# DVE levels in two halves with the first one compared on DVE, G rows issued singly, and POOL's seven levels compared and scaled on POOL

## The chip, the core and the metric

The kernel runs on one core of a Trainium2 chip. Its engines are TensorE (PE, matmul), VectorE (DVE), ScalarE (ACT), GpSimd (POOL) and SyncE (SP), which here issues all the DMAs. Each engine works through its own instruction list in order and waits on semaphores for the others. The metric is the device time of one execution in microseconds; lower is better.

## What is computed

Two linear layers in a row and a residual. The first layer's weights are quantised to a codebook of 32 values, after a LoRA product has been added. Cut to what matters:

```
cb = codebook / max(|codebook|);  scale = exp(scale_log)
lora_delta = lora_B @ lora_A * 0.5                       # 2048 x 2048, rank 64
normalized = (weight + lora_delta).reshape(O, I/128, 128) / scale
idx = searchsorted((cb[:-1] + cb[1:]) / 2, normalized)   # 31 thresholds
w_eff = (cb[idx] * scale).reshape(O, I) + lora_delta
h = x @ w_eff.T                                          # x: 4096 rows of 2048
out = x + h @ W_base.T + b_base + experts(h)             # rank-16 expert part
```

All data are float32. The LoRA rank dimension and the expert part are small against the two large products.

## The kernel before

**Tiling.** The kernel does not compute h. It forms G = w_eff.T times the base weights (with 24 more columns for the experts, 2072 in all) and multiplies x by G. G has 16 blocks of 128 rows, done in four groups of four. For group 0, the start-up loop of `startup()` converts eight halves of weights (q = 0 to 7, each 128 x 1024, two to a block) and multiplies each by eight rows of 128 x 2072 base weights (`rows`, five matmuls of a row into five PSUM banks, in float32). Behind it TensorE multiplies x by the four finished blocks, and the conversion of the other 24 halves runs in the background, paced by `Background`.

**One half of weights.** POOL adds the LoRA delta and multiplies by the reciprocal scale (`normalise`, lines 1288 and 1291). The quantisation is a sum over 31 thresholds of a step times (weight > threshold). ACT makes one-byte masks of 0 or 255 by a saturating activation (`unit`, line 918: `mk`, five buffers). DVE takes 24 of the thresholds, one instruction of 1024 columns each: mask times step plus the running sum `acc`, in PSUM (line 1115; the first one, line 1111, subtracts the weight from the mask's product). Seven thresholds are POOL's: ACT writes a mask of its own for them (`mp`, line 924), POOL scales it (line 1302, `tm`) and adds it to its partial sum `pp` (line 1315). The last DVE instruction of a half adds both sums and the lowest code (line 1122, semaphore `cl`). POOL then multiplies by the scale and adds the delta (`effective`, lines 1323 and 1325, semaphore `we`), behind DVE's first level of the next half. The last half of the loop is finished by DVE itself (`final_weights`).

**LoRA products.** 64 `wide` products of two matmuls (lines 682 and 683) go through one PSUM bank `pd`; each waits until the one before was copied out (semaphore `dl`), by DVE for the first four (line 1099), by ACT for the rest (line 906). SP writes each pair to DRAM and reads the deltas back (lines 496, 505). `delta_places()` says after which (q, j) each one stands.

**Order.** All engines go through one list of events, `walk()`: for each half the levels j = 0 to 23, with the rows of the half before at j = 7 and, at j = 3 of every second half from q = 3, `rows_out`: ACT copies the finished block of G (line 957) and DVE takes its low part (line 1149), which the next block's rows wait for. SP's loads of base weights have a ring of three buffers; a load waits for the row three places earlier. DVE waits for masks in pairs, so its level 3 waits for ACT's mask 4, which ACT writes behind its copies of `rows_out`.

## Time and profile before

| | |
|---|---|
| median of 3 runs | 2389.73 us (2389.25 to 2390.38) |
| profiled execution: span | 2389.1 us |
| busy: PE, DVE, ACT, POOL | 97%, 71%, 60%, 53% |
| base-weight rows of group 0 on PE (line 703) | 560 records, 207.6 us busy |
| idle of POOL before line 1323, for DVE | 173.6 us over the whole run |
| DMA | 442.58 MB, 185 GB/s on average |

The times outside the profile (runs) and its span differ by 0.6 us. Busy shares are means over stages with different limits: in the first 320 us the halves are converted while TensorE has gaps; from there on it is full up to the last stores. A float32 matmul has two records in the trace.

### The profile page before, as it was taken

The numbers are of one execution on the slowest core, as the hardware profiler recorded it, in microseconds if no ns is written. First come the engines' busy times: TensorE is split into PE (matmuls) and PEld (weight loads), VectorE is DVE, ScalarE is ACT, GpSimd is POOL, SyncE is SP. The second block draws the span as 40 slices with busy tenths as digits, with TensorE's granted clock in tenths as the row PEclk, the third lists the DMA queues.
The fourth block names the chain that finished last, engine by engine and source line by source line (L and its number), as shares of the span: only waits on it lengthen the run. The fifth ranks groups of instructions, "written<-read, shape, count | busy, mean of one in ns | idle before, by whom it ended". The sixth has DMA issues, their size and how long they took to land.

```text
span 2389.1 us, 30759 instructions
## 1 busy us (share of the span) xinstructions
PE 2318.9 (97%) x11678; PEld 2102.9 (88%) x11678; DVE 1708.0 (71%) x2021; ACT 1427.1 (60%) x1799; POOL 1270.6 (53%) x704
## 2 busy tenths in 40 slices
PE   3989899999999999999999999999999999999999
PEld 2445479999999999999999999999999989999998
DVE  8899998999978868777868967878873333333333
ACT  7999978989977656665646657566643321111111
POOL 6989847779874437777764436777760000111010
PEclk9989999999999999999999999999999999999999
DMA  5788854443343435766764436667664334545554
GB/s 198 272 274 277 309 208 162 162 166 141 138 149 114 118 116 197 238 230 225 234 219 123 119 105 200 222 232 238 221 208 128 102 96 161 197 180 198 185 195 152
DMA packets 121561, 442.58 MB, mean 185 GB/s; under 512 B 12818, under 2 KB 53330, under 8 KB 84562
## 3 DMA queue, kind: packets, MB, share of 16 engines
q1 hardware_dynamic: 121412, 440.61, 54.4%
q8 instruction: 92, 1.51, 0.3%
q14 instruction: 57, 0.47, 0.1%
HBM read 289.43 MB, written 151.13 MB: 184 GB/s over the span
## 4 chain that ended last, share of the span: by engine, by line
PE 91%; DVE 4%; ACT 3%; POOL 1%; issue 0%; DMA 0%; SPq 0%; DVEq 0%; POOLq 0%; ACTq 0%
PE m L777 20%; PE m L776 20%; PE m L778 20%; PE m L761 8%; PE m L762 8%; PE m L760 8%; PE m L703 4%; DVE acc L1115 3%; ACT mk L918 2%; PE m L806 1%; ACT mp L924 1%; PE pd L682 0%; DMA lb<-in_lb 0%; PE pd L683 0%; ACT ds L906 0%
## 5 line engine op out<-in xcount | busy, mean ns | idle before, releaser
L1115 DVE SCALAR_TENSOR_TENSOR acc<-mk,dj,acc 128x1024 f32<-128x1024 uint8 x736 | 944.9, 1284 | 91.6 <-ACT mk L918 72.1
L776 PE MATMUL m<-gh,xh 128*128 128x384 f32 (+2 forms) x2560 | 903.2, 353 | 0.0
L777 PE MATMUL m<-gl,xh 128*128 128x384 f32 (+2 forms) x2560 | 898.7, 351 | 0.0
L778 PE MATMUL m<-gh,xl 128*128 128x384 f32 (+2 forms) x2560 | 896.0, 350 | 0.0
L918 ACT ACTIVATE mk<-wr,bj 128x1024 uint8<-128x1024 f32 x768 | 843.8, 1139 | 0.7 <-DVE acc L1115 0.7
L776 PEld LDWEIGHTS m<-gh,xh 128*128 128x128 f32 x2560 | 481.6, 188 | 23.5
L778 PEld LDWEIGHTS m<-gh,xl 128*128 128x128 f32 x2560 | 480.9, 188 | 23.6
L777 PEld LDWEIGHTS m<-gl,xh 128*128 128x128 f32 x2560 | 481.4, 188 | 21.2
L1315 POOL TENSOR_TENSOR pp<-pp,tm 128x1024 f32<-128x1024 f32 x192 | 466.4, 2429 | 22.0
L1335 POOL TENSOR_TENSOR xl<-xw,xh 128x512 fp32r<-128x512 f32 x96 | 124.1, 1294 | 564.7 <-ACT xh L972 564.4
L1302 POOL TENSOR_SCALAR tm<-mp,dj 128x1024 f32<-128x1024 uint8 x224 | 258.1, 1152 | 246.5 <-ACT mp L924 235.6
L760 PE MATMUL m<-kh,wh 128*128 128x384 f32 (+2 forms) x936 | 328.8, 351 | 0.0
L762 PE MATMUL m<-kh,wl 128*128 128x384 f32 (+2 forms) x936 | 328.2, 351 | 0.0
L761 PE MATMUL m<-kl,wh 128*128 128x384 f32 (+2 forms) x936 | 328.0, 350 | 0.0
L1169 DVE TENSOR_TENSOR kl<-kw,kh 128x384 fp32r<-128x384 f32 (+2 forms) x234 | 189.1, 822 | 141.2 <-ACT kh L952 140.7
L1163 DVE TENSOR_TENSOR part<-m,part 128x384 f32<-128x384 f32 (+2 forms) x320 | 187.9, 587 | 131.5 <-PE m L778 130.4
L952 ACT ACTIVATE kh<-kw 128x384 fp32r<-128x384 f32 (+2 forms) x234 | 126.8, 548 | 251.8 <-DMA kw<-in_wb 251.2
L924 ACT ACTIVATE mp<-wr,bj 128x1024 uint8<-128x1024 f32 x224 | 255.1, 1139 | 0.1
L972 ACT ACTIVATE xh<-xw 128x512 fp32r<-128x512 f32 x128 | 80.1, 628 | 240.2 <-DMA xw<-in_x 240.2
L703 PE MATMUL m<-rows,wr 128*128 128x384 f32 (+2 forms) x560 | 207.6, 534 | 2.3 <-POOL wr L1325 1.5
L703 PEld LDWEIGHTS m<-rows,wr 128*128 128x128 f32 x560 | 112.2, 201 | 96.3 <-issue 50.6
L760 PEld LDWEIGHTS m<-kh,wh 128*128 128x128 f32 x936 | 175.8, 188 | 8.4 <-POOL wl L1329 0.2
(131 smaller groups left out, 1781.3 us busy)
## 6 DMA issues: line engine op xcount, KB each, us to landing
part<-part SPq DMA_DIRECT2D x192, 1036.0 KB, 6.7
rows<-in_wb SPq DMA_DIRECT2D x61, 1036.0 KB, 4.8
xw<-in_x SPq DMA_DIRECT2D x128, 256.0 KB, 3.2
out<-part SPq DMA_DIRECT2D x31, 1024.0 KB, 4.2
kw<-in_wb SPq DMA_DIRECT2D x138, 192.0 KB, 2.4
wr<-in_w SPq DMA_DIRECT2D x32, 512.0 KB, 8.8
dl<-delta SPq DMA_DIRECT2D x30, 512.0 KB, 5.9
delta<-ds SPq DMA_DIRECT2D x24, 512.0 KB, 3.2
```

The source lines that it names most:

```text
L703: done = e.matmul(R.m[c][:, 0:width(c)], R.wr[raw_of(q)][:, (t % 8) * 128:(t % 8 + 1) * 128], R.rows[r % 3][:, cols(c)], start=t == 0, sto ...
L760: e.matmul(bank[:, 0:w], high, kh, start=t == 0, stop=False)
L761: e.matmul(bank[:, 0:w], high, kl, start=False, stop=False)
L762: done = e.matmul(bank[:, 0:w], low, kh, start=False, stop=t == NB - 1 and not own(b, c))
L776: e.matmul(R.m[c][:, 0:w], xh, gh, start=k == 0, stop=False)
L777: e.matmul(R.m[c][:, 0:w], xh, gl, start=False, stop=False)
L778: done = e.matmul(R.m[c][:, 0:w], xl, gh, start=False, stop=stop and k == n - 1)
L918: e.activation(R.mk[k % NM], w, ACT.Identity, bias=R.bj[:, j:j + 1], scale=GROW).then_inc(S["mk"], 1)
L924: e.activation(R.mp[k % 2], w, ACT.Identity, bias=R.bj[:, NV + i:NV + i + 1], scale=GROW).then_inc(S["mp"], 1)
L1115: e.scalar_tensor_tensor(R.acc, R.mk[k % NM], R.dj[:, j:j + 1], R.acc, ALU.mult, ALU.add).then_inc(S["ac"], 1)
L1302: e.tensor_scalar(R.tm[scaled_level(q, i)], R.mp[k % 2], R.dj[:, NV + i:NV + i + 1], 0.0, ALU.mult, ALU.add).then_inc(S["tm"], 1)
L1315: e.tensor_tensor(R.pp, R.pp if i else R.wr[raw_of(q)], R.tm[scaled_level(q, i)], ALU.add).then_inc(S["pp"], 1)
```

## The change

1. A DVE level becomes two instructions of 512 columns (`HALVES`). Each waits for its own half of the level before, so for the instruction before the last one. The closing instruction is halved too, and `cl` counts two per half of weights.
2. The first level needs no mask: DVE compares the weights with the threshold and multiplies by the step (`tensor_scalar`, `is_gt`, `mult`), from SBUF into PSUM. ACT writes 23 masks per half for DVE.
3. POOL's seven levels need no mask either: POOL compares the float32 weights and multiplies by the step (`spare`). The sum starts with the first two scaled levels, so there are six adds instead of seven; the weight itself is no longer in either sum. ACT writes no `mp`. For the later halves (q from 8) the first of the seven goes into `pp` directly (`spare_base`).
4. `effective` waits for the closing halves themselves.
5. The eight rows of a half are events of their own, at j = 7, 10, 15, 17, 20, 23, 23, 23 (`ROW_AT`), on PE and on SP. For q = 3 to 7 the four LoRA products stand at j = 9, 14, 19, 23 instead of 3 to 6; two of half 2 move to half 1. The second and fourth of each of these halves are copied by DVE (`on_vector`).

```diff
@@ -25,9 +25,11 @@
 NJ = NC - 1
 NP = 7
 NV = NJ - NP
+NA, MK = NP - 1, NV - 1
+HALVES = (slice(0, H // 2), slice(H // 2, H))
 SPARE_AT = (0, 3, 6, 10, 13, 16, 19)
-FIRST_AT, EARLY_AT = (1, 3, 5, 8, 11, 14, 17), (0, 1, 3, 6, 10, 13, 16)
 NORM_AT, SPLIT_EVERY = 8, 6
+ROW_AT, LATE_UNITS = (7, 10, 15, 17, 20, 23, 23, 23), (9, 14, 19, 23)
...
@@ -82,8 +84,9 @@
     for q in range(2 * N0):
         for j in range(NV):
             yield ("unit", q, j)
-            if j == 7 and q:
-                yield ("rows", q - 1)
+            for k in range(8):
+                if ROW_AT[k] == j and q:
+                    yield ("row", q - 1, k)
             if j == 3 and q >= 3 and q % 2:
                 yield ("rows_out", (q - 3) // 2)
         yield ("effect", q)
...
 
-    late = [(0, j) for j in range(6, 22, 2)] + [(1, j) for j in range(1, 7)] + [(2, 3), (2, 4)]
-    late += [(q, j) for q in range(3, 2 * N0) for j in range(3, 7)]
+    late = [(0, j) for j in range(6, 22, 2)] + [(1, j) for j in (1, 2, 3, 4, 5, 6, 9, 14)]
+    late += [(q, j) for q in range(3, 2 * N0) for j in LATE_UNITS]
     late += [(q, j) for q in range(2 * N0, NQ) for j in range(5, NV, 3)]
     return dict(zip(late, range(NDELTA)))
 
@@ -363,7 +366,7 @@
 
 def on_vector(n):
 
-    return n < 4
+    return n < 4 or 16 <= n < 16 + 4 * (2 * N0 - 3) and n % 2 == 1
 
 
...
-        elif what == "rows":
-            for r in range(8 * at[0] + 3, 8 * at[0] + 11):
-                row(r)
-            if at[0] == 2 * N0 - 3:
+        elif what == "row":
+            row(8 * at[0] + 3 + at[1])
+            if at == (2 * N0 - 3, 7):
...
-    def rows(q):
-        b, h = q // 2, q % 2
...
+    def row(q, k):
+        b, t = q // 2, 8 * (q % 2) + k
+        r = NB * b + t
+        if k == 0:
+            e.wait_ge(S["we"], q + 1)
+        if q == 0 and k == 0:
             e.wait_ge(S["dl"], NARROW)
-        for t in range(8 * h, 8 * h + 8):
-            r = NB * b + t
-            e.wait_ge(S[f"r{r % 3}"], 16 * (r // 3 + 1))
-            for c in range(NCH):
...
     def unit(q, j):
-        k, w = NV * q + j, R.wr[raw_of(q)]
+        m, w = MK * q + j - 1, R.wr[raw_of(q)]
         if j == 0:
             e.wait_ge(S["n"], q + 1)
             if q == 0:
                 e.wait_ge(S["bk"], BOOK_READY)
-        if k >= NM:
-            e.wait_ge(S["ac"], k - NM + 1)
-        e.activation(R.mk[k % NM], w, ACT.Identity, bias=R.bj[:, j:j + 1], scale=GROW).then_inc(S["mk"], 1)
-        if j in mask_places(q):
-            i = mask_places(q).index(j)
-            k = NP * q + i
-            if k >= 2:
-                e.wait_ge(S["tm"], k - 1)
-            e.activation(R.mp[k % 2], w, ACT.Identity, bias=R.bj[:, NV + i:NV + i + 1], scale=GROW).then_inc(S["mp"], 1)
+        else:
+            if m >= NM:
+                e.wait_ge(S["ac"], summed((m - NM) // MK, (m - NM) % MK + 1))
+            e.activation(R.mk[m % NM], w, ACT.Identity, bias=R.bj[:, j:j + 1], scale=GROW).then_inc(S["mk"], 1)
...
     def unit(q, j):
-        k = NV * q + j
-        if q >= 2 * N0 or k == 0:
-            e.wait_ge(S["mk"], k + 1)
-        elif j % 2:
-            e.wait_ge(S["mk"], k + 1 + (j < NV - 1))
-        if j == 0:
-            if q:
-                e.wait_ge(S["cl"], q)
-            e.scalar_tensor_tensor(R.acc, R.mk[k % NM], R.dj[:, j:j + 1], R.wr[raw_of(q)], ALU.mult,
-                                   ALU.subtract).then_inc(S["ac"], 1)
-        else:
-            e.wait_ge(S["ac"], k)
-            e.scalar_tensor_tensor(R.acc, R.mk[k % NM], R.dj[:, j:j + 1], R.acc, ALU.mult,
+        w, m = R.wr[raw_of(q)], MK * q + j - 1
+        for h, at in enumerate(HALVES):
+            if j == 0:
+                if h == 0:
+                    e.wait_ge(S["n"], q + 1)
+                    if q == 0:
+                        e.wait_ge(S["bk"], BOOK_READY)
+                if q:
+                    e.wait_ge(S["cl"], 2 * q - 1 + h)
+                e.tensor_scalar(R.acc[:, at], w[:, at], R.u[:, 1:2], R.dr[:, 0:1], ALU.is_gt, ALU.mult).then_inc(S["ac"], 1)
+                continue
+            if h == 0 and q >= 2 * N0:
+                e.wait_ge(S["mk"], MK * q + j)
+            elif h == 0 and j % 2:
+                e.wait_ge(S["mk"], MK * q + min(j + 1, MK))
+            e.wait_ge(S["ac"], summed(q, j - 1) - 1 + h)
+            e.scalar_tensor_tensor(R.acc[:, at], R.mk[m % NM][:, at], R.dj[:, j:j + 1], R.acc[:, at], ALU.mult,
                                    ALU.add).then_inc(S["ac"], 1)
         if j == NV - 1:
-            e.wait_ge(S["ac"], k + 1)
-            if q < 2 * N0 - 1:
-                e.wait_ge(S["mk"], k + 2)
-            e.wait_ge(S["pp"], NP * (q + 1))
-            e.scalar_tensor_tensor(R.wr[raw_of(q)], R.acc, R.cn[:, 0:1], R.pp, ALU.add, ALU.add).then_inc(S["cl"], 1)
+            for h, at in enumerate(HALVES):
+                if h == 0:
+                    e.wait_ge(S["pp"], NA * (q + 1))
+                e.wait_ge(S["ac"], summed(q, j) - 1 + h)
+                e.scalar_tensor_tensor(w[:, at], R.acc[:, at], R.cn[:, 0:1], R.pp[:, at], ALU.add,
+                                       ALU.add).then_inc(S["cl"], 1)
 
     def final_weights():
...
 
+    def spare(q, i, to):
+        n = NV + i
+        e.tensor_scalar(to, R.wr[raw_of(q)], R.u[:, n + 1:n + 2], R.dr[:, n:n + 1], ALU.is_gt,
+                        ALU.mult).then_inc(S["tm"], 1)
+
+    def spare_base(q):
+        e.wait_ge(S["n"], q + 1)
+        e.wait_ge(S["cl"], 2 * q)
+        spare(q, 0, R.pp)
+
...
+
     def spare_scaled(q, i):
-        k = NP * q + i
-        e.wait_ge(S["mp"], k + 1)
-        if k == 0:
-            e.wait_ge(S["bk"], BOOK_READY)
+        if i == 0:
+            e.wait_ge(S["n"], q + 1)
+            if q == 0:
+                e.wait_ge(S["bk"], BOOK_READY)
         if q >= 2 * N0:
-            e.wait_ge(S["pp"], k)
-        elif k >= 2:
-            e.wait_ge(S["pp"], k - 1)
-        e.tensor_scalar(R.tm[scaled_level(q, i)], R.mp[k % 2], R.dj[:, NV + i:NV + i + 1], 0.0, ALU.mult, ALU.add).then_inc(S["tm"], 1)
+            e.wait_ge(S["pp"], NA * q + i - 1)
+        elif i in (2, 3):
+            e.wait_ge(S["pp"], NA * q + 1)
+        elif i > 3:
+            e.wait_ge(S["pp"], NA * q + i - 2)
+        elif q:
+            e.wait_ge(S["pp"], NA * q + i - 1)
+        spare(q, i, R.tm[scaled_level(q, i)])
 
     def spare_added(q, i):
         k = NP * q + i
-        if i == 0:
-            e.wait_ge(S["n"], q + 1)
+        if i == 1:
             if q:
-                e.wait_ge(S["cl"], q)
+                e.wait_ge(S["cl"], 2 * q)
             if q == 2 * N0:
                 e.wait_ge(S["rl"], NB // 2 - FINAL_WHOLE)
-        if i:
-            e.wait_ge(S["pp"], k)
+        else:
+            e.wait_ge(S["pp"], NA * q + i - 1)
         e.wait_ge(S["tm"], k + 1)
-        e.tensor_tensor(R.pp, R.pp if i else R.wr[raw_of(q)], R.tm[scaled_level(q, i)], ALU.add).then_inc(S["pp"], 1)
+        first = R.tm[scaled_level(q, 0)] if i == 1 and q < 2 * N0 else R.pp
+        e.tensor_tensor(R.pp, first, R.tm[scaled_level(q, i)], ALU.add).then_inc(S["pp"], 1)
 
     def effective(q):
         w = R.wr[raw_of(q)]
-        if q < 2 * N0:
-            e.wait_ge(S["ac"], NV * (q + 1) + 1)
-        else:
-            e.wait_ge(S["cl"], q + 1)
+        e.wait_ge(S["cl"], 2 * q + 2)
         e.tensor_tensor(grouped(w, 8), grouped(w, 8), per_group(R.sc, 8 * q, 8), ALU.mult).then_inc(S["ws"], 1)
         e.wait_ge(S["ws"], q + 1)
         e.tensor_tensor(w, w, R.dl[q % 2], ALU.add).then_inc(S["we"], 1)
...
                         spare_scaled(q, i)
-                else:
-                    if (q, i) == (0, 0):
+                        spare_added(q, i)
+                    elif q > 2 * N0:
+                        spare_base(q)
+                elif i == 0:
+                    if q == 0:
                         spare_scaled(0, 0)
                         spare_scaled(0, 1)
-                    if 1 < i + 1 < NP:
+                elif i == 1:
+                    spare_added(q, 1)
+                    spare_scaled(q, 2)
+                else:
+                    if i + 1 < NP:
                         spare_scaled(q, i + 1)
-                spare_added(q, i)
+                    spare_added(q, i)
             if j == NORM_AT and q + 1 < NQ:
                 normalise(q + 1)
             if at == (0, 11):
                 lora_b(1)
         elif what == "effect":
-            if at[0] < 2 * N0:
+            if at[0] < 2 * N0 - 1:
                 spare_scaled(at[0] + 1, 0)
-            if at[0] < 2 * N0 - 1:
                 spare_scaled(at[0] + 1, 1)
-            if at[0] != 2 * N0 - 1:
+            if at[0] == 2 * N0 - 1:
+                spare_base(2 * N0)
+            else:
                 effective(*at)
         elif what == "split":
             split(*at)
```

DVE at the seam of half 0 and half 1 (`wr_49` and `wr_50`: their weights; `mk`: masks). Before:

```order
L1115 SCALAR_TENSOR_TENSOR acc<-mk_143,dj,acc 128x1024
L1115 SCALAR_TENSOR_TENSOR acc<-mk_144,dj,acc 128x1024
L1122 SCALAR_TENSOR_TENSOR wr_49<-acc,cn,pp 128x1024
L1111 SCALAR_TENSOR_TENSOR acc<-mk_145,dj,wr_50 128x1024
L1115 SCALAR_TENSOR_TENSOR acc<-mk_141,dj,acc 128x1024
L1115 SCALAR_TENSOR_TENSOR acc<-mk_142,dj,acc 128x1024
```

Now:

```order
L1116 SCALAR_TENSOR_TENSOR acc<-mk_142,dj,acc 128x512 x2
L1116 SCALAR_TENSOR_TENSOR acc<-mk_143,dj,acc 128x512 x2
L1123 SCALAR_TENSOR_TENSOR wr_49<-acc,cn,pp 128x512 x2
L1109 TENSOR_SCALAR acc<-wr_50,u,dr 128x512 x2
L1116 SCALAR_TENSOR_TENSOR acc<-mk_144,dj,acc 128x512 x2
L1116 SCALAR_TENSOR_TENSOR acc<-mk_145,dj,acc 128x512 x2
```

Each instruction has become two of 512 columns, and the first level of the new half reads weights, threshold `u` and step `dr` and no mask.

TensorE at the start of the rows of half 4 (`wr_53`; `pd` is the LoRA bank, `idn` the unit matrix that closes a block). Before:

```order
L690 MATMUL m<-idn 128x128
L682 MATMUL pd<-las,lbh 128x512
L683 MATMUL pd<-las,lbl 128x512
L682 MATMUL pd<-las,lbh 128x512
L683 MATMUL pd<-las,lbl 128x512
L682 MATMUL pd<-las,lbh 128x512
L683 MATMUL pd<-las,lbl 128x512
L682 MATMUL pd<-las,lbh 128x512
L683 MATMUL pd<-las,lbl 128x512
L703 MATMUL m<-rows_109,wr_53 128x384 x3
L703 MATMUL m<-rows_109,wr_53 128x512
L703 MATMUL m<-rows_109,wr_53 128x408
```

Now, further on in the rows of half 4:

```order
L705 MATMUL m<-rows_109,wr_53 128x408
L684 MATMUL pd<-las,lbh 128x512
L685 MATMUL pd<-las,lbl 128x512
L705 MATMUL m<-rows_107,wr_53 128x384 x3
L705 MATMUL m<-rows_107,wr_53 128x512
L705 MATMUL m<-rows_107,wr_53 128x408
L684 MATMUL pd<-las,lbh 128x512
L685 MATMUL pd<-las,lbl 128x512
L705 MATMUL m<-rows_108,wr_53 128x384 x3
L705 MATMUL m<-rows_108,wr_53 128x512
L705 MATMUL m<-rows_108,wr_53 128x408
L705 MATMUL m<-rows_109,wr_53 128x384 x3
```

The LoRA products stood together ahead of the rows and now stand between them, one pair of matmuls at a time.

SP in the period of half 4 to 5 (`delta<-ds`: a pair of LoRA products written out; `dl<-delta`: a delta read back; `rows`: base weights, ring of three). Before:

```order
L496 DMA delta<-ds_83 128x4x256
L505 DMA dl_137<-delta 128x1024
L496 DMA delta<-ds_84 128x4x256
L511 DMA rows_107<-in_wb 128x2072
L511 DMA rows_108<-in_wb 128x2072
L511 DMA rows_109<-in_wb 128x2072
L511 DMA rows_107<-in_wb 128x2072
L511 DMA rows_108<-in_wb 128x2072
L511 DMA rows_109<-in_wb 128x2072
L511 DMA rows_107<-in_wb 128x2072
L511 DMA rows_108<-in_wb 128x2072
L496 DMA delta<-ds_82 128x4x256
```

Now:

```order
L514 DMA rows_107<-in_wb 128x2072
L514 DMA rows_108<-in_wb 128x2072
L499 DMA delta<-ds_83 128x4x256
L514 DMA rows_109<-in_wb 128x2072
L514 DMA rows_107<-in_wb 128x2072
L514 DMA rows_108<-in_wb 128x2072
L499 DMA delta<-ds_84 128x4x256
L514 DMA rows_109<-in_wb 128x2072
L514 DMA rows_107<-in_wb 128x2072
L514 DMA rows_108<-in_wb 128x2072
L508 DMA dl_136<-delta 128x1024
```

The eight loads stood in one piece behind the copies; now the fourth product's copy-out stands ahead of the last three loads, which are the first three rows of the next half.

## Rows read from the trace of the kernel before

**Rows 1.** Busy by stretch: microseconds (instructions) of PE, PEld, DVE, ACT, POOL; clock, DMA.

```profile
0.00:60.00 60.00, 20.08 (x54) 12.40 (x54) 50.49 (x79) 47.27 (x51) 36.17 (x25) 1.00 0.57 197
...
110.00:160.00 50.00, 44.11 (x120) 23.66 (x119) 47.21 (x41) 49.73 (x54) 46.63 (x27) 0.90 0.82 282
500.00:700.00 200.00, 200.00 (x1061) 190.40 (x1060) 188.26 (x165) 181.08 (x219) 169.91 (x86) 1.00 0.39 143
```

**Rows 2.** DVE in order of time (start, us): first level; closings of halves 0, 4, 7.

```profile
16.93 1.29 DVE L1111 SCALAR_TENSOR_TENSOR acc<-mk,dj,wr 128x1024 f32<-128x1024 uint8 x1
...
56.02 1.28 DVE L1122 SCALAR_TENSOR_TENSOR wr<-acc,cn,pp 128x1024 f32<-128x1024 f32 x1
...
200.95 1.28 DVE L1122 SCALAR_TENSOR_TENSOR wr<-acc,cn,pp 128x1024 f32<-128x1024 f32 x1
...
312.01 1.28 DVE L1122 SCALAR_TENSOR_TENSOR wr<-acc,cn,pp 128x1024 f32<-128x1024 f32 x1
```

**Rows 3.** Chain of work, 160 to 250 us: start, duration, engine and line.

```profile
173.86 29.52 PE m L703 x80
...
204.71 0.85 ACT gh L957 x3
...
206.75 1.03 ACT mk L918
207.80 1.29 DVE acc L1115
209.09 2.48 DVE gl L1149 x5
...
212.87 1.30 DVE acc L1115
214.19 1.30 DVE acc L1115
215.58 1.30 DVE acc L1115
```

**Rows 4.** Groups in 60 to 330 us: busy us, mean ns, idle before.

```profile
L1115 DVE SCALAR_TENSOR_TENSOR acc<-mk,dj,acc 128x1024 f32<-128x1024 uint8 x162 | 208.7, 1289 | 18.2 <-ACT mk L918 8.2
L918 ACT ACTIVATE mk<-wr,bj 128x1024 uint8<-128x1024 f32 x167 | 180.4, 1143 | 0.7 <-DVE acc L1115 0.7
...
L1315 POOL TENSOR_TENSOR pp<-pp,tm 128x1024 f32<-128x1024 f32 x42 | 98.9, 2354 | 0.5
...
L1302 POOL TENSOR_SCALAR tm<-mp,dj 128x1024 f32<-128x1024 uint8 x48 | 54.2, 1130 | 9.8 <-POOL pp L1315 5.0 <-ACT mp L924 4.8
...
L682 PE MATMUL pd<-las,lbh 128*128 128x512 f32 x26 | 16.5, 635 | 23.3 <-ACT ds L906 23.3
...
L1291 POOL TENSOR_TENSOR wr<-wr,rs 128x1024 f32<-128x1024 f32 x7 | 13.3, 1896 | 0.5
...
L1070 DVE TENSOR_TENSOR las<-la,las 64x512 fp32r<-64x512 f32 x2 | 4.1, 2048 | 0.1
```

**Rows 5.** DVE in order of time, 600 to 640 us: levels and copies of 512 columns.

```profile
612.77 0.68 DVE L1158 COPY part<-m 128x512 f32<-128x512 f32 x1
613.37 1.27 DVE L1115 SCALAR_TENSOR_TENSOR acc<-mk,dj,acc 128x1024 f32<-128x1024 uint8 x1
614.56 0.57 DVE L1158 COPY part<-m 128x408 f32<-128x408 f32 x1
```

**Rows 6.** POOL in order of time: effective weights, and behind the last sum.

```profile
96.16 1.90 POOL L1323 TENSOR_TENSOR wr<-wr,sc 128x1024 f32<-128x1024 f32 x1 [1.88 <-DVE acc L1111]
...
127.63 2.21 POOL L1302 TENSOR_SCALAR tm<-mp,dj 128x1024 f32<-128x1024 uint8 x2
```

**Rows 7.** DVE and PE at the last half; loads of rows, median us to landing.

```profile
314.06 0.69 DVE L1131 TENSOR_TENSOR wr<-wr,dl 128x512 f32<-128x512 f32 x1
...
314.80 7.23 PE L722 MATMUL m<-rows,wr 128*128 128x384 f32 x20 [1.12 <-DVE wr L1131]
...
rows<-in_wb SPq DMA_DIRECT2D x57, 1036.0 KB, 4.8
```

More of the change, by code:

```diff
@@ L241, in __init__ @@
         self.mk = [self.take(f"mk{k}", H, U8) for k in range(NM)]
-        self.mp = [self.take(f"mp{k}", H, U8) for k in range(2)]
         at_las = self.top
@@ L690, in one @@
         return e.matmul(bank[:, o:o + 128], R.idn, R.idn, start=False, stop=True)
[L692 to L706 removed]
+    def row(q, k):
[4 more added lines that the diff above has]
+        if q == 0 and k == 0:
+            e.wait_ge(S["dl"], NARROW)
+        e.wait_ge(S[f"r{r % 3}"], 16 * (r // 3 + 1))
+        for c in range(NCH):
+            if t == 0 and b:
+                e.wait_ge(S["lo"], NCH * (b - 1) + c + 1)
+            done = e.matmul(R.m[c][:, 0:width(c)], R.wr[raw_of(q)][:, k * 128:(k + 1) * 128],
+                            R.rows[r % 3][:, cols(c)], start=t == 0, stop=t == NB - 1 and not own(b, c))
+        done.then_inc(S["row"], 1)
+        if t == NB - 1:
             if b == 0:
@@ L858, in tensor_program @@
                 wide(DELTA_AT[at])
-        elif what == "rows":
-            rows(*at)
+        elif what == "row":
+            row(*at)
         elif what == "final":
```

27 lines of the change are left out of this document (10 added, 17 removed), and 2 rows, old and new, of the table COMPUTE.

## The prediction, made before the changed kernel ran

> **What bounds the kernel now.** I read the table by stretches first. From 500 to 700 us TensorE is busy in every microsecond at the full clock; in the first 60 us it is busy for 20.1 us, and from 110 to 160 for 44.1 of 50 [rows 1]. So only the start-up loop can pay: the eight halves q = 0 to 7 of converted weights. Behind it the order of the walk paces DVE, ACT and POOL under a full TensorE (DVE 94% busy, POOL 85%), and cheaper levels there give nothing.
>
> Next the marks of the loop. C(q) is the end of half q's closing instruction (L1122). The first level starts at 16.93; the closings of q = 0, 4 and 7 start at 56.02, 200.95 and 312.01 [rows 2], so C(0) = 57.3, C(4) = 202.2, C(7) = 313.3: seven periods of 36.6 us. The last weights follow on DVE and release TensorE's final rows at 314.80, after 1.12 us of waiting [rows 7]. What lies behind that is full TensorE work, 2389.1 - 314.8 = 2074.3 us, and I carry it over unchanged. The sum is therefore about one mark: when do the final rows start?
>
> Which engine sets the period? ACT writes 24 + 7 masks per half. In the stretch 60 to 330 us 167 level masks took 180.4 us, 1.08 each [rows 4], so 33.5 us a half, plus four copies of LoRA products, its share of the row copies and the gaps while TensorE makes the products: about 36 us, and its busy column in 110 to 160 reads 49.7 of 50 [rows 1]. DVE has 24 levels and a closing; three in a row start at 212.87, 214.19 and 215.58 [rows 3], so by turns 1.32 and 1.39 apart (1.39 where DVE also waits for a mask), 1.36 on average. 23 of these, 1.4 for the first, 1.32 for the closing make 34.0, and every second half 2.48 for the low parts of finished rows [rows 3]. So ACT and DVE are within 2 us of each other. A third thing shows in the chain: TensorE's 8 rows of half 3 take 29.52 us up to 203.4, ACT then copies the finished rows from 204.71, writes its next mask at 206.75, and only then does DVE's fourth level start at 207.80 [rows 3]. TensorE is in the chain through that join, three times (q = 3, 5, 7).
>
> **The change part by part.** *ACT.* It loses 8 of 31 masks per half (the seven of POOL and the first level's), 8.6 us at 1.08. It was at the limit and now has 25 us of masks in a period of 35: this takes it out of the bound, and DVE is next late.
>
> *DVE, the halves.* A level now is two instructions of 512 columns. The gain is that a half does not wait for the one directly before it. How much is that? The 1024-column level takes 1.29 us and a dependent one starts 1.36 later. Where the next instruction doesn't depend on it, that one starts after 1.19 (613.37 to 614.56) [rows 5]. Of this 1024 / 0.96 GHz = 1.067 is columns, which leaves 0.13 fixed. A copy of 512 columns hands over after 0.60 (612.77 to 613.37) [rows 5], so 0.07 fixed; the three-operand form with a per-partition scalar pays 0.06 more. Two bounds for a half level: 0.60 if it hands over like the copy, 0.79 if each half still waits (0.53 + the 0.22 that 1.29 has above its columns + 0.04). A half needs the half before the last, which ended 0.5 us earlier, so I see nothing that holds it, and take 0.53 + 0.13 = 0.66, a level 1.32. That is 0.04 less than now, or 0.9 us per half of weights: the doubled fixed cost eats most of the wait. The first level is a compare with two per-partition scalars; no such row, between 1.20 and 1.58; I take 1.4. Closing: 2 x 0.66. Base of a half: 23 x 1.32 + 1.4 + 1.32 = 33.1.
>
> The Trainium skill (Vector Engine (DVE) Microarchitecture Reference, 5.2 Measured stream behaviour on trn2) gives about 75 ns fixed per instruction after overlap. The copy's row agrees with it, the level's row, at 0.13, does not. By its figure a half would be 0.61, a level 1.22; what that gives is the second rival.
>
> *DVE, what is added.* Nine copies of LoRA products move from ACT to DVE ahead of C(7), and a tenth stands between C(7) and the last weights: 0.6 each by the copy's row, 5.4 + 0.6. The low parts, 3 x 2.48, stay; so do two low halves of the LoRA factor, 2.05 each (4.1 for 2) [rows 4].
>
> *The first half.* 16.9 + 1.4 + 30.4 + four copies of 2.4 + about 1.0 where the ACT copies of j = 14 to 20 wait on TensorE = 52.1; closing, C(0) = 53.4 (now 57.3).
>
> *POOL.* It loses one of seven adds (2.35 us) and the waits for masks, and computes from float32 weights what it scaled from a one-byte mask for 1.13 [rows 4]. I take 1.13 (one input, one output, two operations, as before). From the start of its effective weights to its last partial sum 31.5 us pass now (96.16 to 127.63) [rows 6]; less one add 29.1; then two scaled levels 2.3: a loop of 31.5, under DVE's 33.1. In the first half it starts at 17.7 and has 31.6 us of work: 49.3, under 52.1. The effective weights now wait for the closing itself and not for the level behind it, 1.3 us sooner.
>
> *TensorE and its rows.* 8 rows take 29.5 [rows 3]; four LoRA products per half, 0.5 to 0.64 each [rows 4], now stand between the rows. Half q's rows start at about C(q) + 4.4 (POOL's two effective steps), or, as SP now has the copy-out of the fourth product ahead of the loads of the next rows 0 to 2, and that waits for DVE's copy behind the closing: C(q) + 0.6, issue 0.4 and 0.6, landing 4.8 [rows 7], so C(q) + 6.5. Within the half the third product waits for DVE's copy of the second, behind level 14: C(q) + 20.5, and 23 where low parts come first; TensorE gets there at C(q) + 20.6. This costs 2.5 us in every second half and nothing in the others. In the pair q = 3, 4: C(3) = 159.4, rows of half 3 from 165.9 to 197.1, C(4) = 193.8. ACT copies 2.04 (204.71 to 206.75 now), then a mask of 1.14: DVE's fourth level may start at 200.3 and would have been ready at 198.5. A stall of about 2.0, where it was 1.5. For q = 3 and 7 the same sum gives none.
>
> *The sum.* 7 x 33.1 = 231.7; copies 5.4; low parts 7.5; LoRA 4.1; stalls 2.0 + 1.4 (half 1, where ACT's copy at j = 9 waits for the first row) = 3.4; together 252.1. C(7) = 53.4 + 252.1 = 305.5. Copy 0.6, the two steps behind the closing 1.44 (C(7) = 313.3 to 314.06 + 0.69 now) [rows 7]: final rows at 307.5, against 314.8. TensorE ends the rows of half 6 at about 306.6, so both arrive together. 7.3 us gained: span 2381.8. The runs' median is 0.6 above the span: **2382**.
>
> **The rivals.** *1. POOL's compare is dear (slower side).* Beyond 1.13 + 0.22 a level POOL's loop of 31.5 passes DVE's 33.1 and sets the period. For it: no POOL row compares or reads float32 into one scaled level. The nearest dearer rows are 1.90 and 2.35, with two inputs [rows 4]. At 1.90 the loop is 31.5 + 7 x 0.77 = 36.9, C(0) about 56, periods 37.3 on average with the low parts: C(7) = 317, final rows 319, time 2394. At 2.0 it is 2399; at 2.35, 2416. The Trainium skill (GPSIMD Engine Reference, 7. Performance pitfalls for Q7 kernels) says that a body which compares and selects runs at 2.03 cycles an element unless unrolled, and at 1.03 if so. By this a level would be 0.85 us dearer than 1.13, about 1.98; the first case holds if the built-in one is unrolled. No row here shows which.
>
> *2. Halves hand over like the copy (0.60).* A level is 1.20, DVE's half 30, and TensorE and POOL take over: TensorE has 29.5 + 2 for products a half and its join with the low parts. Start of rows at 57, seven halves, 22 products and three joins: final rows at about 287. Time 2362.
>
> *3. Halves still pay.* A wait for a mask besides the one for the level before costs DVE 0.07 now (1.39 against 1.32) [rows 3]. If each level keeps paying it: 184 x 0.07 = 13, a part of it in time where DVE stalls anyway: 2394. Fully held, 0.79 a half, adds 0.26 x 184 = 48: 2430. Against it: a level behind a copy starts with no gap although it has both waits [rows 5].
>
> *4. The queues entangle.* Products between rows and copy-outs between loads delay TensorE by 2 us more a half; DVE's fourth level then stalls 2 more at each of three joins. 2388. DMA is at a share of 0.82 [rows 1], so loads issued late can land late.
>
> **How the numbers follow.** Forecast 0.45 (2376 to 2388, since 0.01 a half over 400 halves is 4 us). Rival 1: 0.17. Rival 2: 0.13. Rival 3: 0.12. Rival 4: 0.10. Something in the full part, where more instructions crowd DVE: 0.03. A measurement can tell 0.2%, 4.8 us. Faster by more: 0.37 of the forecast, 0.13, 0.02 of rival 4, together 0.52. Within: 0.08 + 0.07 + 0.05 of rival 1 + 0.04 of rival 3 + 0.01 = 0.25. Slower: 0.12 + 0.08 + 0.01 + 0.02 = 0.23. The range 2361 to 2404 leaves out half of rival 2 and the dear ends of rivals 1 and 3, about 0.16.
>
> **What would show it.** DVE: half levels 0.66 apart; 0.60 or 0.70 moves everything. POOL: scaled levels at 1.13 and idle time before its effective weights; no idle there means rival 1. ACT with idle time again in the loop. The closing of half 0 at 52, of half 7 at 304, final rows at 307.5; a wait of DVE's fourth level for a mask in half 5 of 2 us. Behind 345 us TensorE without a gap. I am wrong if POOL is the releaser of the closings, or if TensorE waits for rows' loads.

## The result, and the profile after the change

The change makes the kernel 8.4% slower: 2589.51 us (2587.99 to 2591.04) against 2389.88 (2389.25 to 2390.38), ratio 1.0835 with a 95% interval of 1.082 to 1.0851. The profiled execution has a span of 2589.2 us. The forecast was 2382, with a range up to 2404.

The page of the changed kernel, busy time, POOL by fortieths of the span, and the chain of work that ended last (shares of the span):

```profile
PE 2345.2 (91%) x11678; PEld 2119.2 (82%) x11678; DVE 1739.7 (67%) x2831; ACT 1174.4 (45%) x1533; POOL 1773.3 (68%) x672
...
POOL 7999995899999857499999764799997000001100
...
POOL 53%; PE 39%; issue 5%; DMA 2%; DVE 1%; ACT 0%; SPq 0%; POOLq 0%; DVEq 0%; ACTq 0%
...
L1297 POOL TENSOR_SCALAR tm<-wr,u,dr 128x1024 f32<-128x1024 f32 x200 | 768.3, 3843 | 8.2
...
rows<-in_wb SPq DMA_DIRECT2D x61, 1036.0 KB, 6.5
```

POOL is now over half of the chain, and busy for 90% or more in the second to the sixth slice (each is 64.7 us) and again in most slices up to the thirtieth. The line behind it names why: POOL's compare-and-scale level (L1297) takes 3.84 us on average, where the scaled level from a mask took 1.13 [rows 4]. The loads of rows land after 6.5 us instead of 4.8 [rows 7].

Who waits for POOL, from the waits of the whole span (us in total, times, longest), and the same stretches as in [rows 1]:

```profile
DVE wr L1123 <- POOL pp L1331: 252.2, 27, 18.5
...
PE m L705 <- POOL wr L1338: 108.3, 7, 18.0
```

```profile
0.00:60.00 60.00, 21.82 (x56) 12.92 (x56) 48.00 (x100) 38.67 (x43) 41.94 (x19) 1.00 0.60 206
110.00:160.00 50.00, 32.02 (x85) 16.89 (x84) 33.12 (x50) 23.98 (x21) 49.45 (x18) 0.80 0.55 190
500.00:700.00 200.00, 188.72 (x969) 178.94 (x968) 164.03 (x236) 136.57 (x179) 190.26 (x65) 0.96 0.41 146
```

The closing instruction (L1123) waits for POOL's partial sum, and TensorE's rows wait for POOL's effective weights. In 110 to 160 us POOL is busy for 49.45 of 50 and DVE for 33 (47.2 before). TensorE is busy for 32 us there (44 before), and its granted clock is 0.80, where it was 0.90 [rows 1]. Idle time alone does not explain that: in 0 to 60 us, with 21.8 of 60 us busy, the granted clock is 1.00. And 500 to 700, which was full at clock 1.00, now has 11 us without TensorE.

DVE's order of time shows both what the forecast had right and what it had wrong:

```profile
17.00 1.53 DVE L1109 TENSOR_SCALAR acc<-wr,u,dr 128x512 f32<-128x512 f32 x2
18.43 7.99 DVE L1116 SCALAR_TENSOR_TENSOR acc<-mk,dj,acc 128x512 f32<-128x512 uint8 x12
...
67.56 1.41 DVE L1123 SCALAR_TENSOR_TENSOR wr<-acc,cn,pp 128x512 f32<-128x512 f32 x2 [14.77 <-POOL pp L1331]
...
117.27 1.41 DVE L1123 SCALAR_TENSOR_TENSOR wr<-acc,cn,pp 128x512 f32<-128x512 f32 x2 [8.84 <-POOL pp L1331]
```

Twelve half levels take 7.99 us, the last of them 0.75, so (7.99 - 0.75) / 11 = 0.658 apart: the 0.66 of the forecast. But the closing of half 0 then waits 14.77 us for POOL, and the closings are on average 49.3 us apart (to 412.86 for half 7), not the 33 to 36 of the forecast. POOL's own groups in 60 to 330 us add up to that period:

```profile
L1297 POOL TENSOR_SCALAR tm<-wr,u,dr 128x1024 f32<-128x1024 f32 x39 | 147.6, 3789 | 1.8
L1331 POOL TENSOR_TENSOR pp<-pp,tm 128x1024 f32<-128x1024 f32 x27 | 63.4, 2349 | 0.5
L1331 POOL TENSOR_TENSOR pp<-tm,tm 128x1024 f32<-128x1024 f32 x6 | 14.1, 2346 | 0.0
L1338 POOL TENSOR_TENSOR wr<-wr,dl 128x1024 f32<-128x1024 f32 x6 | 14.0, 2341 | 0.5
```

7 x 3.79 + 6 x 2.35 + 8.5 (two steps of normalising, two of effective weights) = 49.1. The final rows start at 423.19, 108.4 us later than before [rows 7], and from there to the end pass 2166.0 us instead of 2074.3, 91.7 more. So nearly half of the loss lies where the forecast carried the time over unchanged.

### The profile page after: what moved, and what is told of

Read it like the earlier page. It is cut to its first block, busy times and chain, and to the rows that moved or that the text cites. A ratio compares the mean times of both kernels' runs of the same rounds, so it can differ in the third digit from the quotient of the medians.

```text
span 2589.2 us, 31052 instructions
## 1 busy us (share of the span) xinstructions
PE 2345.2 (91%) x11678; PEld 2119.2 (82%) x11678; DVE 1739.7 (67%) x2831; ACT 1174.4 (45%) x1533; POOL 1773.3 (68%) x672
## 4 chain that ended last, share of the span: by engine, by line
POOL 53%; PE 39%; issue 5%; DMA 2%; DVE 1%; ACT 0%; SPq 0%; POOLq 0%; DVEq 0%; ACTq 0%
POOL tm L1297 24%; POOL pp L1331 13%; PE m L762 7%; PE m L764 7%; PE m L763 7%; PE m L779 5%; PE m L778 5%; PE m L780 5%; POOL pp L1297 3%; POOL xl L1348 3%; POOL wr L1338 2%; POOL wr L1290 2%; POOL wl L1342 2%; POOL wr L1336 2%; POOL wr L1293 2%
## 5 line engine op out<-in xcount | busy, mean ns | idle before, releaser
L1116 DVE SCALAR_TENSOR_TENSOR acc<-mk,dj,acc 128x512 f32<-128x512 uint8 x1472 | 1013.4, 747 | 71.0 <-ACT mk L921 70.2
L921 ACT ACTIVATE mk<-wr,bj 128x1024 uint8<-128x1024 f32 x736 | 804.9, 1139 | 85.9 <-DVE acc L1116 84.8
L1297 POOL TENSOR_SCALAR tm<-wr,u,dr 128x1024 f32<-128x1024 f32 x200 | 768.3, 3843 | 8.2
L1331 POOL TENSOR_TENSOR pp<-pp,tm 128x1024 f32<-128x1024 f32 x184 | 441.5, 2400 | 46.4 <-DVE gh L1147 24.3
L705 PE MATMUL m<-rows,wr 128*128 128x384 f32 (+2 forms) x560 | 220.1, 552 | 118.3 <-POOL wr L1338 108.3
L1123 DVE SCALAR_TENSOR_TENSOR wr<-acc,cn,pp 128x512 f32<-128x512 f32 x64 | 45.1, 746 | 252.2 <-POOL pp L1331 252.2
```

The costliest lines, as they stand in the source:

```text
L705: done = e.matmul(R.m[c][:, 0:width(c)], R.wr[raw_of(q)][:, k * 128:(k + 1) * 128], R.rows[r % 3][:, cols(c)], start=t == 0, stop=t == NB ...
L921: e.activation(R.mk[m % NM], w, ACT.Identity, bias=R.bj[:, j:j + 1], scale=GROW).then_inc(S["mk"], 1)
L1116: e.scalar_tensor_tensor(R.acc[:, at], R.mk[m % NM][:, at], R.dj[:, j:j + 1], R.acc[:, at], ALU.mult, ALU.add).then_inc(S["ac"], 1)
L1297: e.tensor_scalar(to, R.wr[raw_of(q)], R.u[:, n + 1:n + 2], R.dr[:, n:n + 1], ALU.is_gt, ALU.mult).then_inc(S["tm"], 1)
L1331: e.tensor_tensor(R.pp, first, R.tm[scaled_level(q, i)], ALU.add).then_inc(S["pp"], 1)
```

## The experiments

Each run is named by the number of its section; the three of section 6 are named by their order. Two theories stood after the result. A: POOL's form is dear and is the whole loss, the rest of the change being worth the forecast's few us. B: the new order of rows, products and loads costs time of its own, hidden under POOL's loss.

**1. ACT writes POOL's masks again; all else as changed.**

```diff
-        e.tensor_scalar(to, R.wr[raw_of(q)], R.u[:, n + 1:n + 2], R.dr[:, n:n + 1], ALU.is_gt,
-                        ALU.mult).then_inc(S["tm"], 1)
...
+        e.wait_ge(S["mp"], k + 1)
+        e.tensor_scalar(to, R.mp[k % 2], R.dj[:, n:n + 1], 0.0, ALU.mult, ALU.add).then_inc(S["tm"], 1)
...
```

> The changed kernel with one part undone: ACT writes the seven masks for POOL again and POOL scales the byte mask (mult, add); DVE halves, first level compared on DVE, single rows, six adds all stay. Theory A (only POOL's compare is dear, the forecast's sum holds for the rest): scaled levels back at 1.13 us, POOL's loop 31.5 us, closing of half 7 near 305, time 2376 to 2390. Rival B (the rest of the change costs time by itself: entangled queues, halves): above 2395. ACT has 30 masks a half at 1.04 to 1.08, 31 to 32.5 us, and stays under DVE's 33 to 36 in A.

2410.19 us (2405.31 to 2412.22), ratio 1.008 (1.0067 to 1.0092). Of the 200 us, 179 go with POOL's form, though ACT has its masks again; 20 stay. So POOL's form is most of the loss, but theory A as expected, 2376 to 2390, is missed: theory B holds for the 20.

**2. The kernel before, with only POOL's compare in place of its masks.**

```diff
-        e.tensor_scalar(R.tm[scaled_level(q, i)], R.mp[k % 2], R.dj[:, NV + i:NV + i + 1], 0.0, ALU.mult, ALU.add).then_inc(S["tm"], 1)
+        n = NV + i
+        e.tensor_scalar(R.tm[scaled_level(q, i)], R.wr[raw_of(q)], R.u[:, n + 1:n + 2], R.dr[:, n:n + 1], ALU.is_gt,
+                        ALU.mult).then_inc(S["tm"], 1)
...
```

> The kernel before with only POOL's part: its seven levels compare float32 weights and multiply by the step on POOL, no masks for POOL from ACT; whole DVE levels, rows in one piece, seven adds as before. Theory A: POOL sets the pace, a half takes 34.5 + 7 x 2.65 = 53 us instead of 36.6, and TensorE waits in the later stretches too: 2590 to 2625, more than the changed kernel by its seventh add. Rival B (the loss needs the other parts as well): clearly under 2560.

2658.39 us (2656.56 to 2660.72), ratio 1.1118 (1.1101 to 1.1135), with 3.78 us a level; more than the 2590 to 2625 expected. POOL's form by itself makes a loss of this size. Alone the edit is worse than with the rest, which saves one add of 2.35 us in each of 32 halves (75 us of POOL; the difference is 69).

**3. What in the instruction is dear?** First the compare made a subtraction:

```diff
-        e.tensor_scalar(to, R.wr[raw_of(q)], R.u[:, n + 1:n + 2], R.dr[:, n:n + 1], ALU.is_gt,
+        e.tensor_scalar(to, R.wr[raw_of(q)], R.u[:, n + 1:n + 2], R.dr[:, n:n + 1], ALU.subtract,
                         ALU.mult).then_inc(S["tm"], 1)
```

> The changed kernel with POOL's compare (is_gt) replaced by a subtraction, everything else equal: float32 weights in, two per-partition scalars, multiply by the step (the sum is no longer the quantised weight). Theory C (the compare operation is what is dear): scaled levels 1.1 to 1.3 us and the time of the forecast, 2376 to 2390. Rivals: float32 input or the second per-partition scalar is dear: levels stay at 3.8 us and the time near 2590.

2590.04 us, ratio 1.0835 (1.0821 to 1.085), level 3.80 us in 60 to 330. The compare is not the cause. Then seven forms side by side in one kernel, twice; each of these two kernels was run once, for the lengths of its instructions and not for its time:

> The changed kernel with POOL's seven levels of each half made by seven different instructions on 1024 columns (the sum is no longer the quantised weight): compare alone with a per-partition scalar; compare and multiply by immediates; max and multiply; subtract and multiply; compare and multiply of a byte input; multiply and then compare; compare and multiply as changed. Theory C (compare is dear by itself): the five with a compare 3 to 4 us, the other two 1.1 to 1.3. Rival D (float32 input): all but the byte input dear. Rival E (per-partition scalars): only the immediates cheap. Rival F (a compare in front of a multiply): multiply then compare cheap or different.

> The changed kernel with POOL's seven levels made by other forms (the sum is no longer the quantised weight), to see what made 1.13 us and what 3.8: multiply and add by immediates on float32; multiply and add by two per-partition scalars; add and multiply; subtract alone; multiply alone; multiply by a per-partition scalar and add an immediate on bytes, as the kernel before; compare and multiply on 512 columns. Theory M (only the pair multiply, add has a quick form): the first, second and sixth 1.1 us, the third 3.8, subtract or multiply alone 2.8 as the compare alone was, 512 columns 1.9. Rival: one operation alone is quick when it is multiply; or the quick form needs the byte input.

Groups of POOL (busy us, mean ns) of the first of the two kernels, over 60 to 2560 us: L1311 is `is_gt, mult` as changed, L1309 `mult, is_gt`, L1305 `subtract, mult`, L1303 `max, mult`, L1307 `is_gt, mult` on bytes, L1301 `is_gt, mult` with immediates, L1299 `is_gt` alone. The first four means are 1.5 to 2.6% above those of the start-up loop, where they are 3.78 to 3.79 us:

```profile
L1311 POOL TENSOR_SCALAR tm<-wr,u,dr 128x1024 f32<-128x1024 f32 x32 | 123.2, 3849 | 2.8
L1309 POOL TENSOR_SCALAR tm<-wr,u,dr 128x1024 f32<-128x1024 f32 x31 | 120.6, 3891 | 2.0
L1305 POOL TENSOR_SCALAR tm<-wr,u,dr 128x1024 f32<-128x1024 f32 x31 | 120.5, 3887 | 0.0
L1303 POOL TENSOR_SCALAR tm<-wr,u,dr 128x1024 f32<-128x1024 f32 x31 | 119.7, 3862 | 1.6
L1307 POOL TENSOR_SCALAR tm<-wr,u,dr 128x1024 f32<-128x1024 uint8 x31 | 119.5, 3856 | 1.8
L1301 POOL TENSOR_SCALAR tm<-wr 128x1024 f32<-128x1024 f32 x31 | 112.8, 3638 | 2.6
...
L1299 POOL TENSOR_SCALAR tm<-wr,u 128x1024 f32<-128x1024 f32 x7 | 19.9, 2843 | 0.0
```

Then of the second, 60 to 330 us: L1305 `subtract` alone, L1307 `mult` alone, L1311 `is_gt, mult` on 512 columns, L1301 `mult, add` and L1303 `add, mult` with two per-partition scalars, L1309 `mult, add` on bytes, L1299 `mult, add` with immediates:

```profile
L1305 POOL TENSOR_SCALAR tm<-wr,u 128x1024 f32<-128x1024 f32 x7 | 20.0, 2850 | 0.0
L1307 POOL TENSOR_SCALAR tm<-wr,u 128x1024 f32<-128x1024 f32 x7 | 19.9, 2846 | 0.0
L1311 POOL TENSOR_SCALAR tm<-wr,u,dr 128x512 f32<-128x512 f32 x7 | 14.5, 2078 | 0.8
L1301 POOL TENSOR_SCALAR tm<-wr,u,dr 128x1024 f32<-128x1024 f32 x7 | 8.7, 1237 | 0.7
L1303 POOL TENSOR_SCALAR tm<-wr,u,dr 128x1024 f32<-128x1024 f32 x7 | 8.4, 1197 | 0.7
L1309 POOL TENSOR_SCALAR tm<-wr,dr 128x1024 f32<-128x1024 uint8 x7 | 7.9, 1122 | 0.7
L1299 POOL TENSOR_SCALAR tm<-wr 128x1024 f32<-128x1024 f32 x6 | 6.3, 1047 | 0.5
```

There are two classes. A pair of `mult` and `add`, in either order, takes 1.05 to 1.24 us whether the input is float32 or bytes and the scalars are immediates or per-partition. Every other pair measured (`is_gt, mult`, `max, mult`, `subtract, mult`, `mult, is_gt`) takes 3.6 to 3.9, and a single operation 2.85, a plain `mult` too. The 1.13 of before was a `mult, add` on bytes whose second operation, an `add` of 0.0, changes nothing in the result; L1309 repeats it at 1.12. That the idle `add` is what makes it quick is argued from float32, where `mult` alone takes 2.85 and `mult, add` 1.05; `mult` alone on bytes was not run. Why there are two classes no run shows.

**4. The order of before put back, on top of run 1** (rows in one piece at j = 7, products at j = 3 to 6, those of halves 1 and 2 in their old places, all but the first four copied by ACT):

```diff
-            for k in range(8):
-                if ROW_AT[k] == j and q:
+            if j == 7 and q:
+                for k in range(8):
                     yield ("row", q - 1, k)
...
-    late = [(0, j) for j in range(6, 22, 2)] + [(1, j) for j in (1, 2, 3, 4, 5, 6, 9, 14)]
-    late += [(q, j) for q in range(3, 2 * N0) for j in LATE_UNITS]
+    late = [(0, j) for j in range(6, 22, 2)] + [(1, j) for j in range(1, 7)] + [(2, 3), (2, 4)]
+    late += [(q, j) for q in range(3, 2 * N0) for j in range(3, 7)]
...
-    return n < 4 or 16 <= n < 16 + 4 * (2 * N0 - 3) and n % 2 == 1
+    return n < 4
```

> The kernel of run e1_masks_back (everything changed but POOL's compare) with the order of rows and LoRA products as before too: all eight rows of a half at j = 7, the products at j = 3 to 6, all but four copied by ACT. What is left of the change: DVE halves, first level compared on DVE, six adds, effective weights behind the closing. Theory Q (the 17 to 20 us that e1_masks_back is over the kernel before are the queues' entanglement: SP's loads behind the copy-outs, TensorE's rows behind products that DVE copies): closings from half 4 no longer late, final rows at 303 to 309, time 2377 to 2384. Rival H (the halved levels or the compare on DVE cost it): stays above 2400.

2385.35 us (2383.17 to 2388.63), ratio 0.9981 (0.9973 to 0.999). Theory B is shown: the new order costs about 25 us (2410.19 - 2385.35). Without it what is left of the change (halves, the first compare, one add less, effective weights behind the closing) gains 5 us on the kernel before, where the forecast had 7.3 for the whole change.

**5. Run 1 with SP's copy-outs of the products moved behind the loads of the rows.**

```diff
-                if n % 2:
+                if n % 2 and 16 <= n < 36:
+                    held.append(n)
+                elif n % 2:
                     delta_out(n)
...
             row(8 * at[0] + 3 + at[1])
+            if at[1] in (3, 7) and held:
+                delta_out(held.pop())
```

> The kernel of e1_masks_back with one thing moved: in halves 3 to 7 SP issues the copy-out of the second product pair behind the loads at j = 17 and that of the fourth behind the last load of the half, so no load of rows waits for a copy of DVE. TensorE's, ACT's and DVE's order stay. If SP's order is all of theory Q: waits of TensorE for rows' loads (19.7 us now) gone, time as e5 would be plus DVE's ten copies, 2382 to 2390. If TensorE's order (product three waits for DVE's copy of product two) is the larger part: still 2398 to 2408.

2393.46 us, ratio 1.0012 (1.0003 to 1.0021), between the two ranges expected: 17 of the 25 us go with the place of two copy-outs a half on SP alone. How they do harm is to be read in run 1, all engines, us 231 to 239 (the half 5 period; DVE's L1109 is the copy of a product, SPq L506 its copy-out, L521 loads of rows):

```profile
221.60 9.96 DVE L1129 SCALAR_TENSOR_TENSOR acc<-mk,dj,acc 128x512 f32<-128x512 uint8 x15
...
223.86 0.71 PE L691 MATMUL pd<-las,lbh 128*128 128x512 f32 x1
...
231.47 0.68 DVE L1109 TENSOR_SCALAR ds<-pd 128x512 f32<-128x512 f32 x1
...
232.18 0.38 SPq L506 DMA_DIRECT2D delta<-ds  x1
...
232.60 4.18 SPq L521 DMA_DIRECT2D rows<-in_wb  x3
...
238.90 7.55 PE L712 MATMUL m<-rows,wr 128*128 128x384 f32 x21 [2.01 <-DMA rows<-in_wb]
```

TensorE made the product by 224.8. DVE copies it at 231.47, when its run of 15 half levels is through; SP, which works in order, holds the copy-out and the three loads behind it until 232.18 and 232.60; the next row lands at 238.9 and TensorE waits. Over 60 to 340 us such waits are 19.7 us in 8 pieces in run 1 and 2.2 in 3 with the copy-outs moved. TensorE's waits for low parts stay, 16.9 us and 17.1.

**6. Which of the three parts of the order?** One at a time, each from a kernel with ACT's masks for POOL. Rows single but products early and on ACT (from run 4):

```diff
-            if j == 7 and q:
-                for k in range(8):
+            for k in range(8):
+                if ROW_AT[k] == j and q:
                     yield ("row", q - 1, k)
```

> The fastest kernel so far (masks for POOL from ACT, rows in one piece, products at levels 3 to 6) with the rows issued singly again, at levels 7, 10, 15, 17, 20, 23, 23, 23; products and who copies them stay. The copy-outs of the products then stand ahead of all loads of rows on SP and no row waits for a late product. If the products' late places and the copy-outs behind them are the whole cost, the single rows cost nothing: 2384 to 2388, and final rows at 309 to 311 us. If rows as events of their own cost something by themselves (they move no instruction of TensorE here, but the loads of SP against the deltas' loads), it shows as 2390 or more.

Two of four products copied by DVE, rows in one piece, products early (from run 4):

```diff
-    return n < 4
+    return n < 4 or 16 <= n < 16 + 4 * (2 * N0 - 3) and n % 2 == 1
```

> The same fastest kernel, with the second and fourth product of each half copied by DVE instead of ACT, as the change has it; rows in one piece, products at levels 3 to 6. Moves 0.6 us twice a half from ACT to DVE, ten copies in five halves. If ACT's 30 masks and its copies set the period there, this relieves ACT by 1.2 us a half and the time is the same or up to 4 us less, 2381 to 2386. If DVE is the one that sets it, ten copies of 0.6 us are 6 us more: 2391. A rival between: TensorE's third and fourth product wait longer for DVE, which sits behind its levels, and the rows start later: 2388 to 2395.

All products copied by ACT, rows single, products late (from run 1):

```diff
-    return n < 4 or 16 <= n < 16 + 4 * (2 * N0 - 3) and n % 2 == 1
+    return n < 4
```

> The changed kernel with POOL's masks from ACT (2410 us), and all four products of each half copied by ACT; rows single, products late between them, SP's copy-outs ahead of loads, all as the change has it. The pairing of single rows with early products gave 2384, and DVE's copies with early products 2409, so two readings are left for the 2410. If the late places of the products are the cause (TensorE gets to them late, the copy-out holds back SP's loads behind it, rows wait), this kernel keeps all of it, and ACT, now waiting for the late products too with its masks behind the wait, comes out at 2405 to 2418. If DVE's copies, which sit behind its levels and hold TensorE at the one bank, are the cause in this order too, it goes back to the 2384 to 2390 of the kernel with early products.

| rows | products | copied by | us | ratio (95%) |
|---|---|---|---|---|
| one piece | early | ACT | 2385.35 | 0.9981 (0.9973 to 0.999) |
| single | early | ACT | 2384.10 | 0.9976 (0.9966 to 0.9986) |
| single | late | ACT | 2390.63 | 1.0001 (0.9992 to 1.0011) |
| one piece | early | ACT, DVE | 2409.27 | 1.0079 (1.0064 to 1.0094) |
| single | late | ACT, DVE | 2410.19 | 1.008 (1.0067 to 1.0092) |

The copies on DVE are the cause: 24 us with early products, 20 with late ones. Single rows cost nothing that can be told, late products 6 with ACT's copies. My reading before this table, that the late places were the cause, falls for most of the sum (it expected 2405 to 2418 for the row that measured 2390.63). 2409.27 is above every range expected for DVE's copies; the first two priced them at their 0.6 us, and the third, which named TensorE's wait, ended at 2395. TensorE in that run (205 to 224 us) shows the true price:

```profile
210.50 0.40 PE L692 MATMUL pd<-las,lbl 128*128 128x512 f32 x1
219.07 0.79 PE L691 MATMUL pd<-las,lbh 128*128 128x512 f32 x1 [8.18 <-DVE ds L1109]
```

The product of 210.9 is copied at 218.33, since DVE first waits for a mask, takes two half levels, the low parts of the finished rows and two half levels more. The next product, and behind it all rows, wait 8.18 us for a 0.69 us copy. TensorE is also slower behind that wait: its granted clock is 0.50 from 215 to 225 us (1.00 from 205 to 210), and the first matmul of a product takes 0.79 us where it took 0.48. Over the loop that is little beside the waits: the rows take 209.7 us in all, against 206.1 with ACT's copies. With late products the delay reaches TensorE by SP's queue instead: with ACT's copies in that order its waits for loads of rows are 2.1 us, where they were 19.7. With ACT's copies TensorE waits too, but for 2.8 us at most (single rows, early products). The second row of the table, single rows with products early, has the lowest time measured here, 0.24% under the kernel before; the 1.25 us between it and the first row is less than either spreads.

**7. Halving by itself: run 4 with levels of 1024 columns, the first one still compared on DVE.**

```diff
-HALVES = (slice(0, H // 2), slice(H // 2, H))
+HALVES = (slice(0, H),)
...
```

> The kernel of e5_old_order with whole DVE levels of 1024 columns again; the first level is still compared on DVE. Against e5 this gives what halving alone is worth: by the pitch of 0.66 a half against 1.36 a level, 0.9 us a half of weights, 7 us over the loop if DVE is what is late, 0 to 3 if ACT's 30 masks and TensorE's join are. So 2381 to 2390.

2387.88 us (2386.86 to 2390.37), ratio 0.9991 (0.9982 to 1.0), against 2385.35 with halves: the halving is worth about 2.5 us, less than the spread of the runs (5.5 us with halves). It is the 0 to 3 of the expectation, for a DVE that is not alone in being late, and not its 7. DVE in order of time, first whole, then (run 4) halved:

```profile
101.11 25.75 DVE L1129 SCALAR_TENSOR_TENSOR acc<-mk,dj,acc 128x1024 f32<-128x1024 uint8 x19
```

```profile
99.64 25.31 DVE L1129 SCALAR_TENSOR_TENSOR acc<-mk,dj,acc 128x512 f32<-128x512 uint8 x38
```

Nineteen levels, 25.75 or 25.31 us: 1.36 a level against 1.33.

**8. The premise of the forecast, made true: POOL computes with `add, mult`.**

```diff
-        e.tensor_scalar(to, R.wr[raw_of(q)], R.u[:, n + 1:n + 2], R.dr[:, n:n + 1], ALU.is_gt,
+        e.tensor_scalar(to, R.wr[raw_of(q)], R.u[:, n + 1:n + 2], R.dr[:, n:n + 1], ALU.add,
                         ALU.mult).then_inc(S["tm"], 1)
```

> The changed kernel with one word other: POOL's scaled level is (weight + threshold) * step in place of (weight > threshold) * step, so what is summed is not the quantised weight. Everything else, ACT without its eight masks too, is as in the change. This is the premise that the forecast was made on, a scaled level of about 1.2 us, and tells what the rest of the forecast was worth. By the pair of forms measured before a level takes 1.20 us: POOL's loop is 7 x 0.07 longer than with byte masks, 32. The forecast's own sum then gives 2382 to 2385. The theory that the order of SP's loads and of the products costs some 25 us wherever ACT's masks are written gives the time of the run with the masks back less what ACT's relief is worth: ACT waited for other engines there, so at most a few us: 2400 to 2408.

2401.49 us (2398.4 to 2404.86), ratio 1.0046 (1.0031 to 1.0061), a level 1.21 us. POOL's form is thus worth 2589.5 - 2401.5 = 188 us. And had POOL's price been right, the forecast of 2382 would still have missed by 19 us: a loss of 0.5% where it had a gain of 0.3%. TensorE's longest waits in this run, 60 to 325 us, and the load on which the final rows wait, from the chain (start, us):

```profile
PE m L705 <- DMA rows<-in_wb: 16.0, 9, 3.0
PE m L705 <- DVE gl L1151: 15.9, 3, 5.4
```

```profile
317.25 6.53 DMA rows<-in_wb
```

## Why the prediction was wrong

*What bounds the kernel, and the full part.* Right while POOL keeps up: behind the start of the final rows pass 2399.9 - 323.92 = 2076.0 us in run 8 and 2383.7 - 309.56 = 2074.1 in the fastest kernel; forecast 2074.3. With the dear form it is 2166.0. Cheaper levels gain nothing there, but dearer ones do cost: POOL stood at 85% in 500 to 700 us [rows 1], so 15% was all the cover there was, and I used the number only for the one direction.

*DVE.* Right: pitch 0.658 for 0.66; the level behind the first one starts 1.43 after it for 1.4; the closing of half 0 starts at 52.65 in run 8 for a forecast of 52.1; an undisturbed period of 33.0 there (89.56 to 122.59) for a base of 33.1. Rivals 2 and 3, 0.60 and a kept wait, are both out. The Trainium skill's 75 ns fixed (Vector Engine (DVE) Microarchitecture Reference, 5.2 Measured stream behaviour on trn2) stays 0.05 us short of this form's step: the run decides for 0.13.

*POOL: the failed step.* "I take 1.13 (one input, one output, two operations, as before)." The level takes 3.79. The likeness I went by, the count of inputs and operations, is not what sets the time; the pair of operations is. The mechanism was rival 1, given 0.17, its place and releaser as described, but its bounds, 1.90 and 2.35, were POOL rows with two inputs, and ended far below. With 3.79 in its own sum, a loop of 31.5 + 7 x 2.66 = 50.1, it comes near the measured 49.3. (Its time at 2.35 leaves the first half out: with it the sum is 2419, not 2416.) The Trainium skill (GPSIMD Engine Reference, 7. Performance pitfalls for Q7 kernels) gives 2.03 cycles an element for a body that compares and selects, 1.03 when unrolled, from which my estimate was 1.98 us; the runs bear out neither the size nor the reason, as `subtract` and a plain `mult` are in the slow class as well.

*Rival 1's second half.* It counted only the start-up. By its sum at 3.79 a level C(7) would be at 420; it is at 414.3. The final rows start at 423.19, 8.9 us after it and not 2.0, because their loads stand on SP behind the fourth product's copy-out; that is 108 us of the loss. The other 92 lie behind, where POOL's cover ran out.

*TensorE, its rows and the queues: the second failed step, a term mis-sized.* The sum has stalls of "2.0 + 1.4 (half 1, where ACT's copy at j = 9 waits for the first row) = 3.4", C(7) = 305.5 and final rows at 307.5. In run 8 C(7) is 315.66 and the final rows start at 323.92: 10.2 us late in the loop and 6.2 more behind it:

```profile
317.60 1.57 DVE L1133 TENSOR_TENSOR wr<-wr,dl 128x512 f32<-128x512 f32 x1
```

```profile
309.47 12.29 PE L705 MATMUL m<-rows,wr 128*128 128x384 f32 x30 [2.25 <-DMA rows<-in_wb]
323.92 7.20 PE L724 MATMUL m<-rows,wr 128*128 128x384 f32 x20 [2.15 <-DMA rows<-in_wb]
```

The first weights are ready at 319.17; TensorE ends the rows of half 6 at 321.8, where the forecast had 306.6, and then waits 2.15 us for a load that lands at 323.78, issued behind the fourth product's copy-out. So of the 6.2 us about 4 is TensorE's own lateness and 2.15 the load. The prediction did have this hold for rows 0 to 2 of a next half, C(q) + 6.5, and left it out for the final rows; by its own figure they start at 312.0. For the second product's copy-out it priced only TensorE's third product (2.5 us in every second half) and not the loads that SP holds behind it. Rival 4 named copy-outs between loads with 2 us a half and a chance of 0.10. Measured, DVE's copies cost 20 us in this order.

*ACT's relief* did come: seven masks fewer a half (run 8 against run 1, which also differ by 0.08 us in the scaled level) gain 8.7 us.

*Still open.* Why late products cost 6 us with ACT's copies is only read from TensorE's waits there for low parts (16.9 us in 3 pieces), not tested by a run. Nor was it tested why loads issued late land later, or why the second of the two steps behind the closing takes 1.57 us in run 8 and 0.69 before [rows 7].
